# Attention on one core: the products with V go from between the two pairs of transposed scores to the step's end, ahead of the products with ones

## The reference

```python
def _L0_attn_ref(x, wq, wk, wv, wo, bo):
    ...
    scores = jnp.einsum('bhqd,bhkd->bhqk', q, k) / jnp.sqrt(jnp.asarray(hd, x.dtype))
    causal = jnp.tril(jnp.ones((S, S), dtype=bool))
    scores = jnp.where(causal, scores, jnp.finfo(x.dtype).min)
    attn = jax.nn.softmax(scores, axis=-1)
    ctx = jnp.einsum('bhqk,bhkd->bhqd', attn, v)
    ...
    return ctx @ wo + bo
```

## The kernel before

| step | width | `entries(0)`, keys | `entries(1)`, keys |
|---|---|---|---|
| 0 | 512 | 128, 128, 128 | transpose, 128, 256 |
| 1 | 384 | 256, 256 | 256, 384, 384 |
| 2 | 256 | 384 | 384 |
| 3 | 128 | 512 | 512 |
| 4 | 512 | 512 | 512, 640 |
| 5 | 512 | 640 | 640, transpose, 640 |
| 6 | 512 | 768 | 768, 768 |
| 7 | 512 | 768 | 896 |
| 8 | 512 | 896, 896 | 896 |
| 9 | 384 | 1024 | 1024 |
| 10 | 256 | none | 1024 |
| 11 | 128 | 1024 | none |

## Time and profile before

### The profile page before, as it was taken

The page is one execution under the profiler, slowest core; times in us unless marked ns, Lnnn a source line. Parts: engine busy times, 40 slices in busy tenths (PEclk is TensorE's granted clock), DMA queues, the critical chain, the costliest instruction groups (busy, mean ns, idle before and its releaser), DMA issues. The chain is left out here.

```text
span 2708.5 us, 40542 instructions
## 1 busy us (share of the span) xinstructions
PE 2485.4 (92%) x12832; PEld 1782.6 (66%) x12832; DVE 1205.7 (45%) x2491; ACT 821.6 (30%) x1499; POOL 916.4 (34%) x1099
## 2 busy tenths in 40 slices
PE   7999699999999995869999997399999979999997
PEld 5888444444444434648888886388888858888886
DVE  3332466666766648921111110767677363111122
ACT  3222144554554551124443432201111012222221
POOL 0000255555545453523333332544261312222221
PEclk9999699999999997979999999699999989999999
DMA  6665635444444505520001011504131152000000
GB/s 244 222 224 194 156 91 121 100 111 105 105 111 107 119 27 178 171 82 32 31 31 46 15 39 44 186 32 155 41 114 47 47 170 83 31 31 31 31 32 32
DMA packets 154492, 255.32 MB, mean 94 GB/s; under 512 B 9648, under 2 KB 47536, under 8 KB 153904
## 3 DMA queue, kind: packets, MB, share of 16 engines
q1 hardware_dynamic: 137712, 208.20, 25.7%
q0 software_dynamic: 6144, 25.17, 2.8%
q10 hardware_dynamic: 10560, 20.97, 2.3%
HBM read 161.50 MB, written 92.27 MB: 94 GB/s over the span
## 5 line engine op out<-in xcount | busy, mean ns | idle before, releaser
L739 DVE CUSTOM_DVE_ANT_0 p_junk<-psum,p_causal 128x896 bf16<-128x896 f32 (+7 forms) x512 | 379.4, 751 | 239.3 <-PE psum L600 232.6
L701 ACT ACTIVATE p_probs<-psum 128x512 f32<-128x512 f32 (+3 forms) x768 | 335.6, 489 | 385.5 <-PE psum L611 385.1
L611 PEld LDWEIGHTS psum<-p_qst,p_kst 98*128 98x128 f32 x768 | 119.5, 190 | 254.9 <-ACT p_probs L701 222.3
L1133 POOL TENSOR_TENSOR p_h_lo<-p_h,p_h_hi 128x512 fp32r<-128x512 f32 x128 | 165.0, 1289 | 338.7 <-ACT p_h_hi L1162 338.7
L523 POOL TENSOR_SCALAR_AFFINE_SELECT p_probs<-p_probs 128x128 f32<-128x128 f32 x512 | 151.3, 304 | 316.6 <-ACT p_probs L701 311.6
L611 PE MATMUL psum<-p_qst,p_kst 98*128 98x512 f32 (+3 forms) x768 | 250.8, 405 | 2.4 <-issue 2.1
L600 PE MATMUL psum<-p_kst,p_qst 96*128 96x512 f32 (+5 forms) x768 | 214.6, 368 | 27.3 <-DMA p_kst<-k_parts 16.6
L1765 POOL CAST p_h<-p_h 128x512 fp32r<-128x512 f16 x128 | 91.1, 712 | 374.3 <-ACT p_h L1789 374.2
L848 PE MATMUL psum<-p_xT_hi,tern 128*128 128x512 f32 x512 | 206.7, 404 | 1.4 <-DVE p_xT_lo L1227 1.4
L848 PE MATMUL psum<-p_xT,p_w_hi 128*128 128x512 f32 x512 | 204.0, 398 | 0.7 <-ACT p_xT L1776 0.7
L1198 PE MATMUL psum<-tern,p_h_hi 128*128 128x512 f32 x512 | 203.1, 397 | 1.5 <-POOL p_h_lo L1133 1.5
(11 more groups left out here) (174 smaller groups left out, 4596.1 us busy)
## 6 DMA issues: line engine op xcount, KB each, us to landing
p_qst<-q_parts SPq DMA_DIRECT2D x96, 256.0 KB, 4.6
p_kst<-k_parts SPq DMA_DIRECT2D x96, 256.0 KB, 6.8
q_parts<-p_qk_out SPq DMA_DIRECT2D x32, 512.0 KB, 2.8
k_parts<-p_qk_out SPq DMA_DIRECT2D x32, 512.0 KB, 2.8
ffn_x<-x SPq DMA_DIRECT2D x12, 1024.0 KB, 5.6
p_x<-in_x_t POOLq DMA_DIRECT2D x8, 1024.0 KB, 6.4
p_raw<-in_f_w POOLq DMA_DIRECT2D x8, 1024.0 KB, 7.7
v_rows<-p_v_out SPq DMA_DIRECT2D x32, 256.0 KB, 4.5
```

The source lines that it names most:

```text
L611: pe.matmul(ST_BANKS[st % 2][:, q0:CH], kst[s][0:KD + 2, g, j * P:(j + 1) * P], qst[s][0:KD + 2, c, g, q0:CH], start=True, stop=True).then ...
L701: act.activation(probs[:, n % 2, g, q0:CH], ST_BANKS[st % 2][:, q0:CH], ACT.Exp, scale=SM_SCALE).then_inc(p_ready, 1)
L739: dve.tensor_tensor_reduce(halves_of(junk[:, which, 0:n]), scores, halves_of(causal[:, SEQ - n:SEQ]), 1.0, FLOOR, ALU.add, ALU.max, rowmax ...
L1133: pool.tensor_tensor(h_lo[:, m % 2, :], h[:, m % 2, :], f32(h_hi[:, m % 2, :]), ALU.subtract).then_inc(hl_done, 1)
```

## The change

In every step that has a step behind it, the call of `with_v` goes from between `entries(0)` and S2 to behind `entries(1)`, directly ahead of `with_ones`. Nothing is added or taken away; waits and counts stay.

```diff
                     scores_T(u, s, n, 0)
                     scores_T(u, s, n, 1)
                     entries(0)
-                    if behind:
-                        with_v(*behind)
                     scores_T(u, s, n, 2)
                     scores_T(u, s, n, 3)
                     entries(1)
                     if behind:
+                        with_v(*behind)
                         with_ones(*behind)
```

## The result

| | before | changed |
|---|---|---|
| median | 2709.89 us (2706.63 to 2710.55, four runs) | 2764.86 us (2763.45 to 2766.06, four runs) |
| ratio | 1 | 1.0205, 95% interval 1.0187 to 1.0223 |
| span of the profiled execution | 2708.5 us | 2764.2 us |
| granted PE clock, mean | 0.959 | 0.956 |

The forecast was 2772 us, with 2742 to 2802 as the range and 0.93 for slower. Direction and range held; the size was 63 us and is 55.

The account below looks back on a forecast made before the run. PE was taken to set the attention's pace. 50 us for 15 units, 5 for the last unit and 8 for clock made 63 on 2710.07, giving 2773, as median 2772 us; range 2742 to 2802.

Parts of the forecast that it names:

- The cover: Attention steps: V's products before S2 cover ACT's exponentials; without them S3 cannot start before S0 + 1.66 us at width 512.
- wait + 0.12 - 0.32: Change per step: S3's wait for ACT, plus 0.12 us uncovered weight load, less 0.32 us saved edges.
- the sum of step 7: Step 7, S3 waits 0.53 us for ACT: +0.33 us, 4.41 in place of 4.08; step 6 given the same.
- The edges: Joints around the products: with both products together, each step with one behind it saves 0.10 + 0.10 + 0.12 = 0.32 us.
- Step 8: Two entries nearly cover ACT (-0.13), but the next entry waits 0.57 us for DVE: +0.42 us, 4.57 to 4.99.
- Step 5: DVE sets this step; V now follows the last entry: +0.90, less 0.22 of extra DVE time, +0.68 us per unit.
- Last unit: No entries to cover ACT: +0.66 us for each of four steps, less for others, +5 us, between 4 and 7.
- The last unit's steps are at full clock: Evidence against the fourth rival: the last unit keeps full PE clock though its steps hold no entries.
- Clock: PE loses clock in step 5 of more units than the present 5 of 15: half of a 15 us bound, +8 us.
- The first (edges win): Rival: 0.32 us saved 191 times, 61 us, and ACT's wait costs nothing: 2648 us, chance 0.04.
- The third, a smaller loss: Rival: DVE's terms fail (step 5 +0.33, step 8 -0.13) and no more clock is lost: 2750 us, chance 0.15.
- The fourth, a clock lost widely: Rival: all units lose clock in step 5, half once more: 2790 us, up to 2805 with further terms, chance 0.15.

Follow-up runs that it names:

- half exponentials: Exponentials cover only the second half of a step's queries: 2710.93 us (1.0005) on the kernel before, 2741.14 us (1.0119) on the changed kernel.
- mixed: Kernel before with another table of entries, V late in steps 2, 3 and 7 to 11 but not in the last unit: 2650.39 us, ratio 0.979.
- experiment 6: Kernel before with another table of score entries per spot: V in the middle 2684.61 us, late in every step 2679.87, late in some steps 2650.39.
- V in the middle: Kernel before with another table of score entries per spot, V left between S1 and S2 in every step: 2684.61 us, ratio 0.9914.

## Why the prediction was right, and where it was off

**The cover.** The step "the products with V cover ACT's answer" held. S3's load at 1.67 for 1.66, 24 us of new idle time before L611, and the wait gone with half exponentials (step 7 at 3.95) show it. The forecasts, most of them wait + 0.12 - 0.32, are within 0.09 us for ten of the twelve steps, and within 0.11 for step 11. In step 6 (+0.41 for +0.33) the number was near and the account incomplete. The prediction worked out DVE's limit for step 8 alone and gave step 6 the sum of step 7; step 6 has the same limit, 2.34 us after S0 and so just behind ACT's, and keeps its loss when ACT's wait is taken away. Step 0 keeps its loss then too.

**The edges.** The saving of 0.32 us was sized from single joints. It shows in full in steps 3, 9 and 10 of the mixed kernel of experiment 6 (0.33 to 0.35). In the changed kernel step 11 is 0.26 shorter, and step 7 with half exponentials 0.14 shorter although S2 still waits a little. Both products take 1.85, for 1.90.

**Step 8.** The second DVE wait came as worked out, 2.58 us after S0 for 2.57, fifteen times, +0.46 for +0.42 (the prediction's own terms, -0.13 and 0.57, make +0.44).

**Step 5.** This is the term that failed. "+0.90, less 0.22" took DVE's chain as fixed. It wasn't: the negation went from 0.66 to 0.175 us, since V's move in step 3 shifts POOL's unrelated work by 0.5 us. In the earlier trace rows the 0.70 us before the transpose contain it, and one row of DVE beside one of POOL in that step would have told: 15 of its 32 negations take over three times what the others do. The term was 8 us of the 50. With 0.19 in its place the sum for 15 units is 43, and 38 was measured; the rest is spread over steps 1, 2, 3, 7, 9, 10 and 11, each 0.04 to 0.11 under its forecast, less 0.12 by which steps 6 and 8 were over.

**Last unit.** +6.5 for +5, to the start of its last step. Its wide steps take 4.02 (forecast 3.99). The rest is one loss of clock:

```profile
1048.01:1053.50 5.49, 4.98 (x21) 1.37 (x20) 1.92 (x4) 2.29 (x6) 5.13 (x3) 0.69 0.12 48
```

This is its step 5, 5.49 us with a granted clock of 0.69, against 4.02. "The last unit's steps are at full clock" was evidence from the kernel before only.

**Clock.** +8 was half of a bound, a choice and not a derivation, and 8.6 came. That is luck. Step 5 of two units of the changed kernel, with its clock whole and without:

```profile
487.86:493.98 6.12, 4.94 (x28) 2.16 (x27) 5.42 (x14) 2.18 (x6) 5.65 (x3) 1.00 0.05 20
440.57:448.31 7.74, 6.56 (x28) 2.56 (x27) 5.39 (x14) 2.17 (x5) 6.52 (x4) 0.78 0.10 36
```

In these two kernels the size per unit (1.6 us) and the place, step 5 with its waits for DVE, are firm; with half exponentials or POOL held back some units lose 2.8. How many units lose it is not. In step 5 it was 5 units before, 10 after, 8 and 11 with half exponentials, 11 with POOL held back, 13 with all entries in the first spot and none where PE waits only 0.22 us before the transpose. But with both products in the middle none lost it either, with a step 5 of 6.59 in which PE's waits for DVE add up to 2.1 us, for 1.2 before. Why one unit loses it and the next, with the same instructions, doesn't, stays open; no run here separates it.

**The rivals.** The first (edges win) needed entries of 0.67 us between S1 and S2. Its condition held: with entries put there the same move is a gain. The third, a smaller loss, came partly true in step 5, but not by its reason, and its other half, step 8 at -0.13, did not: it was +0.46. The fourth, a clock lost widely, happened in the experiment with all entries in the first spot and not here.

## What to carry to other kernels

Work that stands between a producer and the reuse of its buffer is cover; before moving it, work out what else stands there step by step, since the same move was about -5 us with one table of entries and +55 with another. Move it only in the steps where enough is left: here that choice was worth 34 us of the 57 that the fastest kernel gains, 7 of them by POOL and DVE meeting at another point. And look at the durations of small operations on the engine that bounds a step, not at their counts alone: one that is several times its median has met something on another engine, and will change when either is moved.

## What the runs showed of the hardware

**A small DVE operation under a long POOL one.** The two operations on 128x16 elements (the negation and the one behind it) take 0.175 us alone. Beside POOL's operations of 2.85 us on 128x1024 elements their time depends on where in POOL's they start:

| DVE's start after POOL's | DVE's operation lasted | ended |
|---|---|---|
| 0.08 us (POOL held back) | 1.06 us | 1.14 us after POOL's start |
| 0.48 us (before) | 0.66 us | 1.14 us after POOL's start |
| 0.98 us (changed, and V late in step 3) | 0.175 us | 1.16 us after POOL's start |
| 1.17 us (before) | 0.175 us | 1.35 us after POOL's start |
| 1.9 to 2.0 us (POOL held back) | 0.89 to 0.98 us | with POOL's operation |

Each row stands for the 15 units of its run within some 0.1 us. None of these small operations that starts 0.07 to 1.14 us into one of POOL's two comparisons ends before the 1.14 us are over; the one that starts at 0.98 needs its 0.175 us till then anyway and loses nothing. One that starts at 1.17 is left alone, and one that starts at 1.9 or later is held to the end. (A single one started 0.02 us into POOL's and was not held, with both products in the middle.) POOL's third operation (`tern`, 2.36 to 2.39 us) does it to the 128x512 product `p_o_out` (0.69 us alone): started 0.95, 1.39 or 2.09 us after POOL's start, it lasted 1.98, 1.55 or 0.82 and ended 2.91 to 2.93 after it; started 2.28 after, it lasted 0.69 (medians of 15 units: V in the middle and mixed of experiment 6, the kernel before, V late in step 3). What POOL does in each stretch is not visible in the trace, and a start or an end of POOL's in a profile is rougher than the others'.

**Half a microsecond on DVE cost more than itself.** In the kernel before it is 0.3 us in one step of every unit, and goes with 1.55 us of PE's clock in a third of them. V late in step 3 alone, a step that it doesn't shorten by more than 0.04, made the kernel 0.38% faster, and of what differs in its trace the 0.5 us on DVE comes first. That the clock follows from it is an inference from when both went, not shown by itself; the kernel with both products in the middle, which waits more and keeps its clock, speaks against a simple rule.
